# Edge attention on Trainium2: the row normalisation moved from GpSimd to VectorE, and the edge table's products spread over three groups

## The reference

```python
h = jnp.maximum(_layernorm(x, axis=-1), 0.0)          # (x - mean) / sqrt(var + 1e-5), then relu
Xq = (H @ W_lin.T).reshape(bt, n, h, dh)
Xv = (H @ W_val.T).reshape(bt, n, h, dh)
e = jnp.einsum('behd,hd->beh', jax.nn.leaky_relu(Xq[:, src] + Xq[:, dst], 0.2), a)
e = e + jnp.log(A0[src, dst] + EPS)[None, :, None]    # softmax over the edges of one source
Y = jax.ops.segment_sum(attn[..., None] * Xv[:, dst], src, num_segments=n)
return Y @ W_out.T                                     # added to x
```

## Time and profile before

| what | value |
|---|---|
| median of 3 runs | 2062.48 us (2058.55 to 2063.45) |
| the profiled execution | 2061.53 us, its span 2060.0 us |
| busy: TensorE, VectorE, ScalarE, GpSimd | 96%, 61%, 48%, 11% of the span |
| mean granted TensorE clock | 0.981 |
| edge attention, about | 1134 us to 1660 us of the span |

### The profile page before, as it was taken

One profiled execution on the slowest core, in us unless ns is written; L12 is line 12 of the kernel. 1 busy time (PEld: TensorE's weight loads), 2 busy tenths in 40 slices (PEclk: granted clock), 3 DMA queues, 4 the chain that ended last, 5 costly groups with the idle time before them and its releaser, 6 DMA issues. The chain is left out here.

```text
span 2060.0 us, 32417 instructions
## 1 busy us (share of the span) xinstructions
PE 1970.3 (96%) x11982; PEld 1600.4 (78%) x11982; DVE 1248.8 (61%) x2549; ACT 989.9 (48%) x1619; POOL 224.6 (11%) x194
## 2 busy tenths in 40 slices
PE   7999999999999999999999899999999899897998
PEld 6998888888888889888887556657566688686998
DVE  7454665454445455554753766665664588897786
ACT  2554664333333333433332464563636246575996
POOL 1000000000111111011011450110100011100000
PEclk8999999999999999999999999999999999998999
DMA  3101001000100000100002321423314032001232
GB/s 118 55 29 41 0 0 41 0 0 0 41 1 1 0 0 1 32 1 41 41 0 82 133 72 52 145 83 95 102 38 148 26 102 69 22 0 51 83 103 92
DMA packets 81491, 99.99 MB, mean 49 GB/s; under 512 B 7408, under 2 KB 73584, under 8 KB 79088
## 3 DMA queue, kind: packets, MB, share of 16 engines
q1 hardware_dynamic: 81392, 98.65, 14.5%
HBM read 61.78 MB, written 33.55 MB: 46 GB/s over the span
## 5 line engine op out<-in xcount | busy, mean ns | idle before, releaser
L706 ACT ACTIVATE b_gate<-b_pG,b_bias 128x512 f32<-128x512 f32 (+2 forms) x460 | 295.0, 669 | 367.9 <-PE b_pG L55 367.0
L53 PE MATMUL b_pG<-b_xshi,b_whi 128*128 128x512 f32 (+2 forms) x920 | 351.5, 382 | 2.2 <-PEq L299 1.4
L55 PE MATMUL b_pG<-b_xshi,b_wlo 128*128 128x512 f32 (+2 forms) x920 | 351.3, 382 | 0.0
L54 PE MATMUL b_pG<-b_xslo,b_whi 128*128 128x512 f32 (+2 forms) x920 | 351.2, 382 | 0.0
L756 DVE CAST b_xshi<-HT 128x512 fp32r<-128x512 f32 (+3 forms) x130 | 57.3, 483 | 284.8 <-PE b_pG L55 268.3
L53 PEld LDWEIGHTS b_pG<-b_xshi,b_whi 128*128 128x128 f32 x920 | 172.7, 188 | 35.4 <-issue 3.1
L54 PEld LDWEIGHTS b_pG<-b_xslo,b_whi 128*128 128x128 f32 x920 | 172.7, 188 | 32.5
L55 PEld LDWEIGHTS b_pG<-b_xshi,b_wlo 128*128 128x128 f32 x920 | 172.7, 188 | 32.4
L55 PE MATMUL b_pG<-b_hshi,b_wlo 128*128 128x512 f32 (+2 forms) x512 | 194.3, 380 | 0.0
L54 PE MATMUL b_pG<-b_hslo,b_whi 128*128 128x512 f32 (+2 forms) x512 | 194.3, 380 | 0.0
L53 PE MATMUL b_pG<-b_hshi,b_whi 128*128 128x512 f32 (+2 forms) x512 | 194.3, 379 | 0.0
(11 more groups left out here) (366 smaller groups left out, 3986.2 us busy)
## 6 DMA issues: line engine op xcount, KB each, us to landing
a_xt<-in_x SPq DMA_DIRECT2D x16, 512.0 KB, 5.8
h_scratch<-HT SPq DMA_DIRECT2D x4, 2048.0 KB, 6.9
l_x<-in_x SPq DMA_DIRECT2D x16, 512.0 KB, 3.4
l_w<-h_scratch SPq DMA_DIRECT2D x16, 512.0 KB, 5.2
x_scratch<-l_x SPq DMA_DIRECT2D x16, 512.0 KB, 3.3
c_x<-x_scratch SPq DMA_DIRECT2D x32, 256.0 KB, 3.6
x_scratch<-c_x SPq DMA_DIRECT2D x32, 256.0 KB, 2.6
l_x<-x_scratch SPq DMA_DIRECT2D x16, 512.0 KB, 3.8
```

The source lines that it names most:

```text
L53: nc.tensor.matmul(out, w_hi, x_hi, start=first, stop=False)
L54: nc.tensor.matmul(out, w_hi, x_lo, start=False, stop=False)
L55: return nc.tensor.matmul(out, w_lo, x_hi, start=False, stop=last)
L706: nc.scalar.activation(gate[s][:, g, 0:plan.n], pG[s][:, g, 0:plan.n], SIG[g], bias=bias[:, plan.p - 1, 2 * g + s:2 * g + s + 1])\
```

## The change

VectorE normalises all four tiles of a group, with four `tensor_scalar` in place of two. GpSimd keeps the power alone (`root`). `normed` counts once per group instead of twice, and `rstd_ready` likewise. The power of group G waits for `normed` of the group before, since it overwrites `rstd`. The products of the table are spread: three after group 2, three after group 3, two after group 4, and each lot waits for `normed` of its group.

```diff
@@ -950,7 +950,6 @@
     AHEAD = 2
     HG = GG // 2
     NH = QG // HG
-    NT = 2
     with ExitStack() as ctx:
         sb, ps = allocator(nc, ctx)
         tab = tables.tab
@@ -1089,18 +1088,11 @@
                 nc.gpsimd.memset(lin[:, :], 0.0).then_inc(sem["half_set"], 1)
                 pool.wait_ge(sem["half_set"], 2)
 
-                def normalise(q, m):
+                def root(q, m):
                     G = NJ * q + m
                     pool.wait_ge(sem["var_eps"], G + 1)
+                    wait(pool, sem["normed"], G)
                     nc.gpsimd.tensor_tensor(rstd[:, :], ve[:, :], mhalf[:, :], ALU.pow).then_inc(sem["rstd_ready"], 1)
-                    pool.wait_ge(sem["rstd_ready"], 2 * G + 1)
-                    xn = hst[m % 2][:, :, :].rearrange("p k (a d) -> p (k a) d", d=D)
-                    shape = [P, GT - NT, D]
-                    nc.gpsimd.tensor_tensor(xn[:, NT:, :], xt[m % 2][:, NT:, :],
-                                            mv[:, NT:, 0:1].to_broadcast(shape), ALU.subtract).then_inc(sem["rstd_ready"], 1)
-                    pool.wait_ge(sem["rstd_ready"], 2 * G + 2)
-                    nc.gpsimd.tensor_tensor(xn[:, NT:, :], xn[:, NT:, :], rstd[:, NT:].unsqueeze(2).to_broadcast(shape),
-                                            ALU.mult).then_inc(sem["normed"], 1)
 
                 def make_pairs(first, end):
                     for n in range(first, end):
@@ -1113,16 +1105,18 @@
 
                 def body(q, last=False):
                     for m in range(3, NJ if last else NJ + 3):
-                        normalise(q, m)
-                        if isinstance(q, int) and q == 0 and m == 3:
-                            make_pairs(3, NP)
-
-                normalise(0, 0)
-                normalise(0, 1)
-                normalise(0, 2)
+                        root(q, m)
+                        if isinstance(q, int) and q == 0 and m in (3, 4):
+                            pool.wait_ge(sem["normed"], m + 1)
+                            make_pairs(3 * (m - 2), min(3 * (m - 1), NP))
+
+                root(0, 0)
+                root(0, 1)
+                root(0, 2)
                 pool.wait_ge(spilled[0], 16)
                 pool.wait_ge(spilled[1], 16 * (SPILLS - 1))
                 pool.wait_ge(tables.made, ONE_HOT)
+                pool.wait_ge(sem["normed"], 3)
                 make_pairs(0, 3)
                 body(0)
                 with pool.Fori(1, NQ - 1) as q:
@@ -1150,7 +1144,7 @@
 
                 def turn(q, m):
 
-                    pe.wait_ge(sem["normed"], 2 * (NJ * q + m + 1))
+                    pe.wait_ge(sem["normed"], NJ * q + m + 1)
                     xn = hst[m % 2][:, :, :].rearrange("p k (a d) -> p (k a) d", d=D)
                     for t in range(GT):
                         for k in range(KD):
@@ -1481,7 +1475,7 @@
                 def measure(q, m):
                     G = NJ * q + m
                     dve.wait_ge(sem["x1_done"], G + 1)
-                    wait(dve, sem["rstd_ready"], 2 * G)
+                    wait(dve, sem["rstd_ready"], G)
                     V.memset(ve[:, :], EPS)
                     for t in range(GT):
                         last = V.bn_stats(st[:, t, :], xt[m % 2][:, t, :])
@@ -1490,7 +1484,7 @@
                 def moments(q, m):
                     G = NJ * q + m
                     dve.wait_ge(sem["stats"], 2 * G + 1)
-                    wait(dve, sem["normed"], 2 * G)
+                    wait(dve, sem["normed"], G)
                     V.memset(unused[:, :], 0.0)
                     for t in range(GT):
                         last = V.bn_aggr(mv[:, t, :], st[:, t, :])
@@ -1500,9 +1494,9 @@
 
                 def normalise(q, m):
                     G = NJ * q + m
-                    dve.wait_ge(sem["rstd_ready"], 2 * G + 1)
+                    dve.wait_ge(sem["rstd_ready"], G + 1)
                     xn = hst[m % 2][:, :, :].rearrange("p k (a d) -> p (k a) d", d=D)
-                    for t in range(NT):
+                    for t in range(GT):
                         last = V.tensor_scalar(xn[:, t, :], xt[m % 2][:, t, :], mv[:, t, 0:1],
                                                rstd[:, t:t + 1], ALU.subtract, ALU.mult)
                     last.then_inc(sem["normed"], 1)
```

## The result

The changed kernel takes 2043.3 us, the median of four runs (2042.51 to 2044.07), against 2062.14 for the kernel before beside it: 0.9907 of its time, 95% interval 0.9894 to 0.9921, 18.8 us. Two later comparisons gave 0.9916 (0.9902 to 0.9929) both.

What follows compares the result with a forecast made beforehand. TensorE, 96% busy, was taken to wait on VectorE's normalised rows, slowed by taking turns with GpSimd. Gains 9.0 + 0.4 + 2.42 + 0.79 + 2.6 = 15.2 us gave 2047.2 us against the median, range 2043.5 to 2052.5.

Steps and rivals of the forecast that it cites:

- the tile term: Ten ordinary groups: four tiles on VectorE gain 0.90 us each, between 0.55 and 0.95; 9.0 us in all.
- The groups behind a scan: Groups 6, 10 and 14, behind a softmax scan: normalising on VectorE gains 0.88 us each, 2.6 in all.
- 2.42 us forecast for the addition: Group 4: with products spread, VectorE's addition of epsilon no longer waits for the run of five; gain 2.42 us.
- The 0.79 for the clock: Group 4 to 5: TensorE's clock dip costs 0.79 us and goes with the idle time.
- Opening and group 2 together: Groups 0 to 2: more VectorE tiles in the opening, masks ending earlier; gain 0.4 us, between -0.2 and 0.9.
- none after it: Sign: the whole gain lies inside the edge attention, with none after it.
- The lower end of the range: 2043.5 us: upper bounds of 0.95 per group and 0.9 for the opening, with runs 2 us under the median.
- B: Normalised rows: TensorE or ScalarE takes over the wait, gain only 10.8 us, 2051.7; chance 0.12.
- C: Group 4 still meets a product, so 3.2 us of addition and clock stay, 2050.4; chance 0.03.
- D: Normalising on VectorE: a tile costs 1.2 us of itself, so the kernel is slower, 2088.8; chance 0.02.
- E: Something outside the chain, a load or store, paces the groups; only 3.6 us gained, 2058.9; chance 0.03.

Runs made afterwards that it cites:

- before_warm: Kernel before, plus nine matmuls nobody reads (fillers) ahead of group 3's `turn_back`, where TensorE waits for the masks: 2060.23 us, ratio 0.9995.
- no_hold: Changed kernel without the products' wait for the normalised group (`normed`): 2071.76 us, ratio 1.0058 to the kernel before.
- cuts_late_warm: Changed kernel with masks moved to the fourth group, eleven unread filler matmuls in the opening and five before group 2's `turn_back`: 2040.53 us, ratio 0.9897.
- opening_shared: Changed kernel with groups 0 and 1 normalised as before, two tiles on each engine: 2043.12 us, ratio 0.9915.
- nt3: Kernel before with three tiles on VectorE and one on GpSimd, in place of two and two: 2056.86 us, ratio 0.998.
- norm_only: Changed kernel with the last five products in one run behind group 3, not spread: 2048.57 us, ratio 0.9942 to the kernel before.

## Why the prediction was right, and where it was wrong

**The step that failed** is the size of the tile term, 0.90 us per ordinary group. It measured 1.01, over its own upper bound of 0.95: 1.1 us more over ten groups. With 0.90 the changed kernel would have been at 2044.4 us, inside the range. An omission is larger in this comparison: outside group 4 the sum puts nothing for TensorE's clock. Behind group 5 the clock accounts for 3.0 us of the difference between the two traces, ahead of it for 1.5 us won and 2.3 lost (both below). With a miss of 0.2 us the side of the bound is luck: the repeats gave 2043.12 and 2044.46.

**The tiles.** The chain of one group was read rightly, and so was the cause of the 2.35 us. The term was mis-sized: "I take a gain of 0.90 us, between 0.55 and 0.95". It is 1.01 us from power to power (18.90 to 17.89). The four tiles took 1.38 us, not 1.40, so their end alone moved 0.97. I had let TensorE hold `project` back to 1235.20, taking the end of the `gather` row, 1234.41, as the earliest start of `turn`. After the change `turn` starts 0.57 us behind the start of the `gather` (1228.23 to 1228.80), although that row is 0.73 long. These rows overlap; from a start the next start has to be counted, as I did for the transposes alone. The groups behind a scan gained 0.8 to 0.9, close to the 0.88 taken (64.74 to 63.91 from group 6 to 7). Over the ten ordinary groups the term was about 1.1 us short.

**The products.** 2.42 us forecast for the addition, 2.42 measured (2.58 to 0.16). The 0.79 for the clock went too (19.69 to 17.88, of which 1.01 is the tiles). `before_warm` shows 18.87 there with the wait in place, so this part of the gain isn't certain in each execution. The hold costs GpSimd what I took, a wait of 1.5 us with nothing behind it but the product. What it saves I had not priced, and that was the larger number: `no_hold` shows 28.7 us.

**The masks and the opening.** "Opening and group 2 together: 0.4 us." The masks end 0.6 us earlier relative to the power, as forecast. What I left out is the clock behind them: the kernel before has 1.2 GHz there, the changed one hasn't, 1.5 us. The first window is of before, the others of after:

```profile
1184.00:1186.00 2.00, 2.00 (x6) 1.61 (x6) 1.88 (x5) 1.08 (x2) 0.00 (x0) 0.50 0.00 0
```

```profile
1148.00:1150.00 2.00, 2.00 (x9) 0.20 (x8) 1.94 (x6) 0.00 (x0) 0.00 (x0) 0.50 0.78 200
1184.00:1186.00 2.00, 1.71 (x12) 1.55 (x13) 1.91 (x5) 0.37 (x1) 0.00 (x0) 1.00 0.00 0
```

In turn the opening lost 2.55 us in this trace, forecast as 0.2. The clock took 2.3 to 2.4 of them: in `cuts_late_warm`, with no such stretch there, the opening from group 0 to group 2 takes 28.49 us, 0.14 more than before. The two nearly cancel. That the idle time brings the clock down behind the masks, `before_warm` supports with one trace; it isn't proof, since the stretch of group 4 stayed away there with its idle time in place. Why the clock stays up in the changed kernel, whose wait there is a little longer (2.39 us against 2.05), is open. So is whether the change makes the opening's slow stretch certain: with four tiles there it came in every trace without fillers, with the opening of before in two of four, and in the one of `opening_shared`.

**The size of the range.** The account stands 3.7 us over the forecast of 15.2. Of that, 0.9 are the tiles of groups 3 to 14; 1.5 the dense part that was slow before by chance; and 1.5 the part behind the last power, where the tiles of group 15 were to bring 0.9 and 2.4 came. The front, up to group 3's power, brought 0.2 less than forecast.

The 1.5 us behind the last power lie outside the edge attention, where I had written "none after it". There both kernels do the same work, and TensorE goes through a stretch at 1.2 GHz: 20.5 us long before (from 1887 us), 17.1 after (from 1869). Its end, before and after, at about the same place in the work:

```profile
1904.00:1908.00 4.00, 4.00 (x22) 3.86 (x21) 0.00 (x0) 2.69 (x4) 0.27 (x1) 0.58 0.02 4
```

```profile
1886.00:1890.00 4.00, 4.00 (x33) 3.84 (x32) 0.10 (x1) 3.52 (x7) 0.31 (x1) 0.95 0.01 4
```

It was the long one in all four traces with two tiles on each engine, and the short one in seven of nine with four tiles on VectorE and in `nt3`. So it isn't plain scatter, though why it is shorter is open. Other stretches come and go there too: the two traces of the unedited kernel before differ by 1.4 us behind the last power by themselves (498.1 and 496.7).

The lower end of the range doesn't follow from its own terms either: 0.95 in ten groups and 0.9 for the opening make a gain of 16.2 us, which with 2 us of scatter is 2043.3 from the profiled execution and 2044.3 from the median. I had given the changed kernel 2 us of scatter and the kernel before none, though its three runs covered 4.9 us. In the later comparisons, with 15 runs each, the kernel before stands at 2060.9 to 2061.6, and the gain at 17 to 18 us.

**The rivals.** B fell: no wait of TensorE or ScalarE took the place. C fell in the changed kernel, and `norm_only` shows its mechanism at 4.0 us, near its 3.2. D fell by L1500 at 0.41 us. E fell: the loads moved with `turn` (from 4.99 to 4.44 us behind the power).

## What to carry to other kernels

Work shared between VectorE and GpSimd wasn't halved here: VectorE's `tensor_scalar` in SBUF and GpSimd's operations took turns, so giving all of it to the faster engine was faster with each tile that moved. A long GpSimd operation that nobody is waiting for belongs behind the short VectorE operation on the critical path, by an explicit wait, and VectorE's operations of one-off set-up belong where no such operation runs. Where an operation took three times what the same form takes elsewhere in the trace, it was waiting, and its twin was the price to plan with.

## What the hardware showed

With GpSimd's operation starting 0.04 us after VectorE's first tile of group 5, the tile still took 1.23 us:

```profile
1232.33 1.23 DVE L1506 TENSOR_SCALAR l_w<-l_x,c_mv,c_rstd 128x256 f32<-128x256 f32 x1 [1.12 <-POOL c_rstd L1095]
```

So the one that starts first in the record needn't be the one that goes first. The Trainium skill, "SBUF — State Buffer", section "Who interferes with whom", says that whoever issues first holds the shared ports for its whole operation. That the other is blocked for a whole operation, `no_hold` bears out to 0.1 us; who was first can't be read from the starts. Stretches of TensorE at 1.2 GHz in the edge attention cost 0.8 to 2.3 us each, in the groups lay around or behind its waits (2.05 us for the masks, 2.73 in group 4), and moved from one execution and one kernel to the next; an edit that filled one idle place saw another appear. A gain of 1 to 2 us is better read from distances inside the trace, since the times of single runs of the kernel before covered 4 to 7 us.
